# Four float32 column-tile products in place of three fp32r products in the attention's projections

## The chip, the cores and the metric

The kernel runs on one core of a Trainium2 chip, as one program of five engines: TensorE (PE, matrix products), VectorE (DVE), ScalarE (ACT), GpSimd (POOL) and SyncE (SP, which here issues every DMA). The engines run side by side and meet by semaphores. The metric is the device time of one execution in microseconds (us), lower is better.

## What is computed

The reference, cut to what matters. The input `x` is (2, 2048, 512) in float32.

```python
def _mhsa(X, ln_g, ln_b, Wq, bq, Wk, bk, Wv, bv, Wo, bo):       # 16 heads of 32
    Xn = (X - mu) * rsqrt(var + EPS) * ln_g + ln_b
    Q, K, V = (split_heads(Xn @ W + b) for W, b in ((Wq, bq), (Wk, bk), (Wv, bv)))
    scores = einsum('bhqd,bhkd->bhqk', Q, K) / sqrt(32)          # causal mask
    AV = einsum('bhqk,bhkd->bhqd', softmax(scores), V)
    return AV.swapaxes(-2, -3).reshape(...) @ Wo + bo

def _ffn(x, ...):                                                # fp4 weights, 512 -> 2 x 1408 -> 512
    gate, up = split(x @ w_gu.T)
    y = (silu(gate) * up) @ w_down.T
    return y / sqrt(mean(y * y) + 1e-6)

x = x + 0.5 * _ffn(_layernorm(x))
x = x + _mhsa(_layernorm(x))
x = x + 0.5 * _ffn(_layernorm(x))
```

## The kernel before

The program has eight stages in a row on every engine (`tensor_program` and its like): the first FFN over 8 token tiles of 512 (`Ffn` with phase 0, which also decodes the weights and keeps them in DRAM as `dg` and `dd`), then for each of two batches the projections Q, K, V (`Qkv`), the attention (`Att`) and the output projection (`Out`), and last the second FFN. Each stage has an order written out once (`order`), which every engine walks through and of which it takes its own steps; waits are explicit (`wait_ge` on a named signal at a key). A step of one engine queues behind all its earlier steps.

**Projections.** A projection is a product of 512 by 512. The PE multiplies fp32r operands, and to keep precision each operand is split into a high part (the value rounded to fp32r) and a low part (the rest), and a product is the sum of three matmuls, high x high, high x low and low x high, accumulated in one PSUM bank. This goes for Xn (`xh`, `xl`), Wq, Wk, Wv (`wh`, `wl`), the attention's result (`Out.ah`, `al`) and Wo (`Out.wh`, `wl`). The contraction of 512 is four chunks of 128 rows, `c` from 0 to 3, so one output tile of 128x512 is twelve matmuls (`qkv_project`, `out_pe`).

For each token tile `tt` of 512 (four per batch), `Qkv.order` gives: eight feature tiles (K and Q in turn, 128 features by 512 tokens) and between them the 48 VectorE steps of the next token tile's two norms; then four value tiles (128 tokens by 512 features), each followed by one `turn` of the next token tile. A `turn` is one chunk of Xn: PE transposes four 128x128 blocks into bank 0 or 1, ScalarE applies gain and bias and writes `xnt`, VectorE copies it to `xh` and subtracts for `xl`. Before token tile 0 the four turns stand alone with three `split` steps, in which ScalarE rounds a weight of 128x2048 to `wh` and VectorE subtracts for `wl`. A finished feature tile is copied by ScalarE to `q32` (with bias), cast to fp16 by VectorE and its rest made by GpSimd. The value tiles of token tile 3 are not done there but in the attention's order, in 16 parts of one chunk each (`value_part`), each followed by one `max` unit.

**Attention.** For each group of four heads and each query tile, PE makes scores twice: once for the row maxima (`max`, VectorE reduces them), once transposed for the exponential (`score`, ScalarE). It needs copies of Q and K stacked by DMA (`stack_sp`). `weigh` multiplies the exponentials by V and `total` sums them, both in float32 with 32 stationary columns per head, the four heads to the four quarters of 32 partitions of one bank:

```python
for j in range(4):
    h = 4 * hg + j
    e.wait_ge(*t.exp_done.at((b, n, j)))
    k = e.matmul(AV[32 * j:32 * j + 32, off:512], p.v[:, kt, 32 * h:32 * h + 32],
                 t.E[n % NE][:, j, off:512], start=kt == 0, stop=kt == 4 * qt + 3)
```

The order mixes `max` units and small steps (`parts`: `invert`, VectorE's reciprocals, and the splits `wo_split` and `av_split`) into the scores by a count of work, in `advance`. `wo_split` splits Wo after step (2, 3, 0), `av_split` the first 512 tokens of the result after step (3, 2, 2).

**Output.** `out_pe` makes 16 tiles of 128 tokens by 512. The splits of the tokens 512 to 2047 stand in `out_act` and `out_dve`. VectorE adds residual and bias (`y_made`) and does the next stage's norm beside it; SP stores the tile. In batch 1, SP also loads the second FFN's weights: for each of 11 column blocks one piece of gate and up (`dg`) and one of down (`dd`), 512 KB each, where their memory is free. Blocks 4 to 7 of `dg` wait for the end, since `Out.wh` and `Out.wl` lie there, and blocks 5 to 8 of `dd` for tile 11, since `ah[0]` and `al[0]` lie there.

## Time and profile before

| | us |
|---|---|
| median of three runs | 2980.32 |
| lowest and highest | 2968.59, 2982.92 |
| the profiled execution | 2964.9 |
| its span | 2963.1 |

| busy in the span | us | share |
|---|---|---|
| PE matmul | 2716.4 | 92% |
| PE weight load (beside matmuls) | 1623.7 | 55% |
| VectorE | 2157.6 | 73% |
| ScalarE | 1381.1 | 47% |
| GpSimd | 1494.4 | 50% |

Rows of the timeline give the start in us from the span's start, the busy time of the merged instructions, the engine, the line of the helper that issued them, the operation with its operands and shape, and in brackets how long the engine was idle before and for whom it waited. `pp` and `ps` are PSUM banks, `sb` is SBUF. "128*32 128x512 f32" is a matmul with 128 rows and 32 stationary columns, and 512 columns that stream through. fp32r operands are shown as f32 too; the three products of the projections are the "128*128 128x512 f32". Busy time holds the modelled end of the last matmul, so the distance between two starts tells more than it does. PEld is the load of stationary operands.

### The profile page before, as it was taken

To read this page: it belongs to the slowest core of one execution; us is meant where nothing else is said; L and a number is where in the kernel's file an instruction comes from. 1 tells how busy PE (TensorE), PEld (TensorE's weight loads), DVE (VectorE), ACT (ScalarE), POOL (GpSimd) and SP (SyncE) were. 2 spreads that over 40 slices of the span, in tenths; PEclk is the share of its full clock that TensorE was granted. 3 is DMA by queue.
4 is the path that set the end of the run, shared out by engine and by line. 5 is a ranking of instruction groups with operands and counts; after the bars stand their busy time and mean duration, and the time that the engine had idled before them with its cause. 6 is when DMAs were issued, how large, how long until landed. Compare 5 with 4: busy or idle time off the path is not lost.

```text
span 2963.1 us, 39754 instructions
## 1 busy us (share of the span) xinstructions
PE 2716.4 (92%) x14559; PEld 1623.7 (55%) x14559; DVE 2157.6 (73%) x3834; ACT 1381.1 (47%) x2667; POOL 1494.4 (50%) x1015
## 2 busy tenths in 40 slices
PE   6799999997998999988899899999988999999998
PEld 4677777775773333322277523332324777777776
DVE  8877777777758777777287587777763777777765
ACT  4444554544213555555522245555554354544554
POOL 5555555553222665555732145555557355555554
PEclk8999999998999999999999999999999999999999
DMA  2022201121022010200140300211003401111101
GB/s 58 15 88 75 113 33 35 43 81 62 29 50 54 5 45 5 59 5 2 37 150 29 89 16 5 45 30 35 4 3 141 172 15 43 43 43 43 43 29 43
DMA packets 75713, 142.12 MB, mean 48 GB/s; under 512 B 18783, under 2 KB 22394, under 8 KB 75390
## 3 DMA queue, kind: packets, MB, share of 16 engines
q1 hardware_dynamic: 75518, 139.58, 15.0%
q8 instruction: 115, 1.88, 0.3%
q14 instruction: 80, 0.66, 0.1%
HBM read 74.00 MB, written 37.22 MB: 38 GB/s over the span
## 4 chain that ended last, share of the span: by engine, by line
PE 55%; DVE 22%; ACT 9%; issue 6%; POOL 2%; SPq 1%; DMA 1%; POOLq 0%; ACTq 0%; DVEq 0%
PE pp L94 42%; PE ps L94 13%; DVE sb L109 9%; ACT sb L100 8%; DVE sb L115 3%; DVE sb L106 3%; DVE sb L103 2%; DVE sb L121 2%; POOL sb L103 2%; SPq L133 1%; DVE sb L118 1%; DVE sb L112 1%; DMA sb<-xa 1%; PE ps L97 0%; DVE sb L124 0%
## 5 line engine op out<-in xcount | busy, mean ns | idle before, releaser
L94 PE MATMUL pp<-sb,sb 128*128 128x512 f32 (+8 forms) x11154 | 2221.4, 435 | 130.3 <-ACT sb L100 33.9
L103 POOL TENSOR_TENSOR sb<-sb,sb 128x512 f32<-128x512 f32 (+6 forms) x998 | 1486.9, 1507 | 1453.4 <-ACT sb L100 594.1
L94 PEld LDWEIGHTS pp<-sb,sb 128*128 128x128 f32 (+3 forms) x11154 | 1196.3, 143 | 855.8 <-ACT sb L100 196.7
L100 ACT ACTIVATE sb<-pp 128x512 f32<-128x512 f32 (+4 forms) x1434 | 674.2, 548 | 546.7 <-PE pp L94 528.7
L94 PE MATMUL ps<-sb,sb 128*128 128x512 f32 (+5 forms) x2862 | 765.9, 362 | 72.3 <-DVE sb L109 25.1
L100 ACT ACTIVATE sb<-sb 128x512 f32<-128x512 f32 (+3 forms) x468 | 300.9, 649 | 680.2 <-DVE sb L109 559.5
L94 PEld LDWEIGHTS ps<-sb,sb 128*128 128x128 f32 (+3 forms) x2862 | 382.0, 148 | 413.7 <-DVE sb L115 197.8
L115 DVE TENSOR_REDUCE sb<-ps 128x1 f32<-128x512 f32 (+3 forms) x754 | 488.4, 670 | 156.4 <-PE ps L94 154.7
L109 DVE SCALAR_TENSOR_TENSOR sb<-ps,sb,sb 128x512 f32<-128x512 f32 x437 | 321.5, 745 | 139.1 <-PE ps L94 121.3
L109 DVE SCALAR_TENSOR_TENSOR sb<-pp,sb,sb 128x512 f32<-128x512 f32 x443 | 324.4, 743 | 119.6 <-PE pp L94 106.2
L115 DVE TENSOR_REDUCE sb<-pp 128x1 f32<-128x512 f32 (+2 forms) x366 | 243.0, 664 | 80.2 <-PE pp L94 79.5
L100 ACT ACTIVATE sb<-pp,sb 128x512 f32<-128x512 f32 x325 | 218.7, 678 | 135.7 <-PE pp L94 114.7
L100 ACT ACTIVATE sb<-ps,sb 128x512 f32<-128x512 f32 x299 | 198.1, 686 | 94.6 <-PE ps L97 90.2
L118 DVE RECIPROCAL sb<-pp 128x64 f32<-128x64 f32 x256 | 114.5, 508 | 99.0 <-PE pp L94 99.0
L103 DVE TENSOR_TENSOR sb<-sb,sb 128x512 fp32r<-128x512 f32 (+4 forms) x165 | 131.6, 822 | 8.8 <-ACT sb L100 6.5
L109 DVE SCALAR_TENSOR_TENSOR sb<-sb 128x4 f32<-128x4 f32 x288 | 106.2, 369 | 6.1
L106 DVE TENSOR_SCALAR sb<-sb 128x4 int32<-128x4 int32 (+2 forms) x233 | 91.7, 410 | 24.4 <-ACT sb L100 20.4
L103 DVE TENSOR_TENSOR sb<-pp,sb 128x512 f32<-128x512 f32 (+1 forms) x95 | 65.0, 688 | 52.4 <-PE pp L94 30.1
L112 DVE CAST sb<-sb 128x512 f16<-128x512 f32 (+2 forms) x128 | 58.6, 458 | 57.6 <-ACT sb L100 56.3
L100 ACT ACTIVATE sb<-ps 128x512 fp32r<-128x512 f32 (+1 forms) x73 | 43.0, 591 | 113.3 <-PE ps L94 73.5
L121 DVE BATCH_NORM_STATS2 sb<-sb 128x6 f32<-128x512 f32 x128 | 86.6, 677 | 11.6 <-DMA sb<-L_attn_X 6.5
L109 DVE SCALAR_TENSOR_TENSOR sb<-sb,sb,sb 128x512 f32<-128x512 f32 x64 | 79.5, 1282 | 0.5
(19 smaller groups left out, 360.9 us busy)
## 6 DMA issues: line engine op xcount, KB each, us to landing
sb<-sb SPq DMA_DIRECT2D x192, 128.0 KB, 2.4
sb<-L_attn_X SPq DMA_DIRECT2D x64, 256.0 KB, 4.0
sb<-xa SPq DMA_DIRECT2D x64, 256.0 KB, 5.3
sb<-xc SPq DMA_DIRECT2D x64, 256.0 KB, 4.3
xa<-sb SPq DMA_DIRECT2D x32, 256.0 KB, 2.0
xc<-sb SPq DMA_DIRECT2D x32, 256.0 KB, 3.7
out<-sb SPq DMA_DIRECT2D x32, 256.0 KB, 2.0
dg<-sb SPq DMA_DIRECT2D x11, 512.0 KB, 8.7
```

What stands on the lines that cost most here:

```text
L94: return self.e.matmul(*a, **k) if self.e else self
L100: return self.e.activation(*a, **k) if self.e else self
L103: return self.e.tensor_tensor(*a, **k) if self.e else self
L106: return self.e.tensor_scalar(*a, **k) if self.e else self
L109: return self.e.scalar_tensor_tensor(*a, **k) if self.e else self
L112: return self.e.tensor_copy(*a, **k) if self.e else self
L115: return self.e.reduce_max(*a, **k) if self.e else self
L118: return self.e.reciprocal(*a, **k) if self.e else self
L121: return self.e.bn_stats(*a, **k) if self.e else self
L133: return self.e.dma_start(*a, **k) if self.e else self
```

## The change

All splits of the four projections are gone, with their buffers and signals. A chunk of a product is now `product`: four float32 matmuls, each with 32 of the 128 stationary columns, written to the quarter of 32 partitions that belongs to these columns. ScalarE writes Xn straight to `xnt`, now a whole token tile and double, and takes over the waits for its memory. The weights are multiplied as they are loaded. SP loads Wq, Wk and Wv for batch 0 together, once the first FFN's token tile 6 has left their memory. The attention's order loses `wo_split` and `av_split`, eight subtractions and eight copies per batch, and `Out` loses twelve of each. As less memory is taken in the output, SP loads 20 pieces of the second FFN's weights with the first ten stores of batch 1, and two, `dg` of blocks 2 and 3, after the last store.

```diff
--- before.py
+++ after.py
@@ -815,35 +815,31 @@
             q = p.qkv
             e.wait_ge(*f.turned.at((NT - 1, KC - 1)))
             q.load_sp(e, 0, 0)
-            e.wait_ge(*f.gu_done.at((0, IC - 1, KC - 1, 1)))
-            for n in (1, 0):
+            e.wait_ge(*f.gu_done.at((NT - 2, IC - 1, KC - 1, 0)))
+            for n in (1, 0, 2):
                 q.weight_sp(e, 0, n)
-    if f.ph == 0:
-        e.wait_ge(*f.stored.at(NT - 1))
-        p.qkv.weight_sp(e, 0, 2)
-    else:
-        e.wait_ge(*f.stored.at(NT - 1))
+    e.wait_ge(*f.stored.at(NT - 1))
+
+
+def product(e, out, left, right, start, stop):
+
+    for j in range(0, 128, 32):
+        k = e.matmul(out[j:j + 32, :], left[:, j:j + 32], right, start=start, stop=stop)
+    return k
 
...
 class Qkv:
     def __init__(self, p):
         self.p = p
-        self.raw = [[p.at([128, KC, D], F32, o) for o in raw]
-                    for raw in ((A0 + 24576, A0 + 32768, XR0), (C0 + 8192, C0, XR0))]
         o = QS0 + 32768
-        self.wh = [p.at([128, KC, D], F32R, o + 16384 * i) for i in range(3)]
-        self.wl = [p.at([128, KC, D], F32R, o + 16384 * i + 8192) for i in range(3)]
-        self.xnt = [p.at([128, 512], F32, KP0 + 16384 + 2048 * i) for i in range(2)]
+        self.w = [p.at([128, KC, D], F32, o + 8192 * i) for i in (1, 0, 2)]
         self.q32 = [p.at([128, 512], F32, KP0 + 20480 + 2048 * i) for i in range(2)]
-        xo = [KP0, o + 49152]
-        self.xh = [p.at([128, KC, 512], F32R, xo[i]) for i in range(2)]
-        self.xl = [p.at([128, KC, 512], F32R, xo[i] + 8192) for i in range(2)]
+        self.xnt = [p.at([128, KC, 512], F32, x) for x in (KP0, o + 49152)]
         self.x_in = p.sign("q_x_in", 16)
         self.w_in = [p.sign(f"q_w_in{n}", 16) for n in range(3)]
-        names = ("normed", "turned", "xnt_made", "xh_made", "xl_made", "wh_made", "wl_made", "proj_done", "q_wide",
-                 "q_hi", "q_lo", "v_made")
-        (self.normed, self.turned, self.xnt_made, self.xh_made, self.xl_made, self.wh_made, self.wl_made,
-         self.proj_done, self.q_wide, self.q_hi, self.q_lo, self.v_made) = (p.sign("q_" + x) for x in names)
+        names = ("normed", "turned", "xnt_made", "proj_done", "q_wide", "q_hi", "q_lo", "v_made")
+        (self.normed, self.turned, self.xnt_made, self.proj_done, self.q_wide, self.q_hi, self.q_lo, self.v_made) = (
+            p.sign("q_" + x) for x in names)
         self.src = p.xa.rearrange("(b n t p) d -> b n t p d", b=B, t=4, p=128)
...
-        e.dma_start(self.raw[b][n][:, :, :], w).then_inc(*self.w_in[n].up(b))
+        e.dma_start(self.w[n][:, :, :], w).then_inc(*self.w_in[n].up(b))
...
     def order(self, b):
-        yield "turn", 0, 0
-        yield "turn", 0, 1
-        yield "split", 1
-        yield "turn", 0, 2
-        yield "turn", 0, 3
-        yield "split", 0
-        yield "split", 2
+        for c in range(KC):
+            yield "turn", 0, c
         yield "load", 1
...
     for c in range(KC):
-        e.wait_ge(*q.xl_made.at((b, tt, c)))
-        e.matmul(bank, lh(c), rh(c), start=c == 0, stop=False)
-        e.matmul(bank, lh(c), rl(c), start=False, stop=False)
-        k = e.matmul(bank, ll(c), rh(c), start=False, stop=c == KC - 1)
+        e.wait_ge(*q.xnt_made.at((b, tt, c)))
+        k = product(e, bank, left(c), right(c), c == 0, c == KC - 1)
         if c < KC - 1:
             yield
     k.then_inc(*q.proj_done.up((b, *key)))
...
-    e.wait_ge(*q.wl_made.at((b, 2)))
-    yield from qkv_project(e, p, b, tt, ("values", tt, tb), lambda c: q.xh[i][:, c, c0], lambda c: q.xl[i][:, c, c0],
-                           lambda c: q.wh[2][:, c, :], lambda c: q.wl[2][:, c, :])
+    e.wait_ge(*q.w_in[2].at(b))
+    yield from qkv_project(e, p, b, tt, ("values", tt, tb), lambda c: q.xnt[i][:, c, c0], lambda c: q.w[2][:, c, :])
...
         if what == "turn":
             tt, c = at
             e.wait_ge(*q.turned.at((b, tt, c)))
-            if tt or c >= 2:
-                last = (b, tt, c - 2) if c >= 2 else (b, tt - 1, c + 2)
-                e.wait_ge(*q.xl_made.at(last))
+            if tt >= 2:
+                e.wait_ge(*q.proj_done.at((b, "values", tt - 2, 3)))
+            elif tt == 1 and b:
+                for s in p.out.stored:
+                    e.wait_ge(*s.at((0, 3)))
             elif b == 0:
                 e.wait_ge(*p.f[0].w_out.at("all"))
-            e.activation(q.xnt[c % 2][:, :], p.b[c % 2], ACT.Identity, scale=p.bias[:, 0, c:c + 1],
+            e.activation(q.xnt[tt % 2][:, c, :], p.b[c % 2], ACT.Identity, scale=p.bias[:, 0, c:c + 1],
                          bias=p.bias[:, 1, c:c + 1]).then_inc(*q.xnt_made.up((b, tt, c)))
-        elif what == "split":
-            n = at[0]
-            e.wait_ge(*q.w_in[n].at(b))
-            if n == 2 and b:
-                for s in p.out.stored[0:2]:
-                    e.wait_ge(*s.at((0, 3)))
-            if n == 0:
-                e.wait_ge(*q.wl_made.at((b, 1)))
-            e.activation(q.wh[n][:, :, :], q.raw[b][n][:, :, :], ACT.Copy).then_inc(*q.wh_made.up((b, n)))
...
     q = p.qkv
     gens = {}
     for what, *at in q.order(b):
-        if what == "turn":
-            tt, c = at
-            i = tt % 2
-            e.wait_ge(*q.xnt_made.at((b, tt, c)))
-            if c == 0 and tt >= 2:
-                e.wait_ge(*q.proj_done.at((b, "values", tt - 2, 3)))
-            elif c == 0 and tt == 1 and b:
-                for s in p.out.stored:
-                    e.wait_ge(*s.at((0, 3)))
-            elif c == 0 and tt == 0 and b == 0:
-                e.wait_ge(*p.f[0].w_out.at("all"))
-            e.tensor_copy(q.xh[i][:, c, :], q.xnt[c % 2][:, :]).then_inc(*q.xh_made.up((b, tt, c)))
-            e.wait_ge(*q.xh_made.now())
-            e.tensor_tensor(q.xl[i][:, c, :], q.xnt[c % 2][:, :], q.xh[i][:, c, :], ALU.subtract).then_inc(
-                *q.xl_made.up((b, tt, c)))
-        elif what == "split":
-            n = at[0]
-            e.wait_ge(*q.wh_made.at((b, n)))
-            e.tensor_tensor(q.wl[n][:, :, :], q.raw[b][n][:, :, :], q.wh[n][:, :, :], ALU.subtract).then_inc(
-                *q.wl_made.up((b, n)))
...
             if n < N:
                 if steps[n] == (2, 1, 0):
                     out.append(("wo",))
-                if steps[n] == (2, 3, 0):
-                    parts += [("wo_split", c) for c in range(KC)]
-                if steps[n] == (3, 2, 2):
-                    parts += [("av_split", 0, c) for c in range(KC)]
...
-        self.wraw = p.at([128, KC, D], F32, C0 + 8192)
-        self.wh, self.wl = (p.at([128, KC, D], F32R, C0 + 16384 + 8192 * i) for i in range(2))
-        self.ah = [p.at([128, KC, 512], F32R, x) for x in (KP0, o)]
-        self.al = [p.at([128, KC, 512], F32R, x + 8192) for x in (KP0, o)]
+        self.w = p.at([128, KC, D], F32, C0 + 8192)
         self.xr = [[p.at([128, 512], F32, (o + 32768 if i < 12 or b == 0 else XR0 - 24576) + 2048 * i)
                     for i in range(16)] for b in range(B)]
         self.w_in = p.sign("o_w_in", 16)
         self.x_in = [p.sign(f"o_x_in{n}", 16) for n in range(16)]
         self.stored = [p.sign(f"o_stored{q}", 16) for q in range(4)]
-        (self.wh_made, self.wl_made, self.ah_made, self.al_made, self.biased, self.done, self.y_made) = (
-            p.sign("o_" + x) for x in ("wh_made", "wl_made", "ah_made", "al_made", "biased", "done", "y_made"))
...
-def out_wo_act(e, p, b, c):
-    o = p.out
-    e.wait_ge(*o.w_in.at(b))
-    e.activation(o.wh[:, c, :], o.wraw[:, c, :], ACT.Copy).then_inc(*o.wh_made.up((b, c)))
...
-def out_wo_dve(e, p, b, c):
-    o = p.out
-    e.wait_ge(*o.wh_made.at((b, c)))
-    e.tensor_tensor(o.wl[:, c, :], o.wraw[:, c, :], o.wh[:, c, :], ALU.subtract).then_inc(*o.wl_made.up((b, c)))
...
-def out_split_act(e, p, b, q, c):
-    o = p.out
-    e.wait_ge(*p.att.normed.at((b, c, q)))
-    if q >= 2:
-        e.wait_ge(*o.done.at((b, 4 * (q - 2) + 3)))
-    elif q == 1:
-        e.wait_ge(*p.att.exp_done.at((b, 159, 3)))
-    else:
-        e.wait_ge(*p.att.exp_done.at((b, p.att.last_step(2), 3)))
-    e.activation(o.ah[q % 2][:, c, :], p.avn[:, c, 512 * q:512 * q + 512], ACT.Copy).then_inc(*o.ah_made.up((b, q, c)))
-
-
-def out_split_dve(e, p, b, q, c):
-    o = p.out
-    e.wait_ge(*o.ah_made.at((b, q, c)))
-    e.tensor_tensor(o.al[q % 2][:, c, :], p.avn[:, c, 512 * q:512 * q + 512], o.ah[q % 2][:, c, :],
-                    ALU.subtract).then_inc(*o.al_made.up((b, q, c)))
...
+        e.wait_ge(*o.w_in.at(b))
         for c in range(KC):
-            e.wait_ge(*o.al_made.at((b, q, c)))
-            e.wait_ge(*o.wl_made.at((b, c)))
-            e.matmul(p.b[n % 8], o.ah[i][:, c, c0], o.wh[:, c, :], start=c == 0, stop=False)
-            e.matmul(p.b[n % 8], o.ah[i][:, c, c0], o.wl[:, c, :], start=False, stop=False)
-            k = e.matmul(p.b[n % 8], o.al[i][:, c, c0], o.wh[:, c, :], start=False, stop=c == KC - 1)
+            e.wait_ge(*t.normed.at((b, c, q)))
+            k = product(e, p.b[n % 8], p.avn[:, c, 128 * n:128 * n + 128], o.w[:, c, :], c == 0, c == KC - 1)
...
         q, tb = divmod(n, 4)
-        if tb == 0 and q < 3:
-            for c in range(KC):
-                out_split_dve(e, p, b, q + 1, c)
...
     for n in range(16):
         e.wait_ge(*p.f[0].stored.at(4 * b + n // 4))
         e.dma_start(o.xr[b][n][:, :], o.src[b, n // 4, n % 4]).then_inc(*o.x_in[n].up(b))
-    e.wait_ge(*o.wl_made.at((b, 3)))
     if b == 0:
         for n in (1, 0, 2):
             p.qkv.weight_sp(e, 1, n)
     else:
         e.wait_ge(*p.f[0].w_out.at("all"))
-    first = [x for i in (0, 1, 2, 3, 4, 8, 9, 10) for x in ((i, 0), (i, 1)) if x not in ((4, 0), (8, 1))]
+    first = [x for i in range(IC) for x in ((i, 0), (i, 1)) if x not in ((2, 0), (3, 0))]
     for n in range(16):
         if b == 1:
             for i, u in first[2 * n:2 * n + 2]:
                 load_piece_sp(e, p, f, i, u)
-            if n == 12:
-                e.wait_ge(*o.done.at((1, 11)))
-                for i in range(5, 9):
-                    load_piece_sp(e, p, f, i, 1)
         e.wait_ge(*o.y_made.at((b, n)))
         e.dma_start(o.dst[b, n // 4, n % 4], o.xr[b][n][:, :]).then_inc(*o.stored[n // 4].up((b, 3)))
     if b == 1:
-        for i in range(4, 8):
+        for i in range(2, 4):
             load_piece_sp(e, p, f, i, 0)
```

On PE at the start of the projections of batch 0, the order before (`sb_141` and `sb_143` are the high and low part of Wk, `sb_132` and `sb_135` those of Xn):

```order
L97 MATMUL ps<-sb_49,sb_102 128x128
L97 MATMUL ps<-sb_49,sb_103 128x128
L94 MATMUL pp<-sb_141,sb_132 128x512
L94 MATMUL pp<-sb_143,sb_132 128x512
L94 MATMUL pp<-sb_141,sb_135 128x512
```

And now, with `sb_126` Wk, `sb_125` Wq, `sb_127` Wv and `sb_130` Xn:

```order
L97 MATMUL ps<-sb_49,sb_102 128x128
L97 MATMUL ps<-sb_49,sb_103 128x128
L94 MATMUL pp<-sb_130,sb_126 32x512 x16
L94 MATMUL pp<-sb_130,sb_125 32x512 x16
L94 MATMUL pp<-sb_130,sb_126 32x512 x16
```

Twelve matmuls per tile have become sixteen of 32 rows of output.

On VectorE late in the attention of batch 0 (`sb_161` is the low part of the attention's result, the other rows are maxima and reciprocals), before:

```order
L118 RECIPROCAL sb_149<-pp 128x64
L115 TENSOR_REDUCE sb_151<-ps 128x1
L118 RECIPROCAL sb_149<-pp 128x64 x7
L103 TENSOR_TENSOR sb_161<-sb_118,sb_159 128x512 x4
L115 TENSOR_REDUCE sb_151<-pp 128x1
L115 TENSOR_REDUCE sb_151<-ps 128x1 x2
```

And now:

```order
L118 RECIPROCAL sb_136<-pp 128x64
L115 TENSOR_REDUCE sb_138<-ps 128x1
L118 RECIPROCAL sb_136<-pp 128x64 x7
L115 TENSOR_REDUCE sb_138<-pp 128x1
L115 TENSOR_REDUCE sb_138<-ps 128x1 x2
```

The four subtractions between the reciprocals and the next maxima are gone; the rest stands as it stood.

## Rows read from the trace of the kernel before

**Rows 1.** The page: its span, and the chain that ended last by engine.
```profile
span 2963.1 us, 39754 instructions
...
PE 55%; DVE 22%; ACT 9%; issue 6%; POOL 2%; SPq 1%; DMA 1%; POOLq 0%; ACTq 0%; DVEq 0%
```

**Rows 2.** Busy times in the attention of batch 0; columns stand in the first line.
```profile
core 0: us, PE busy (x) PEld busy (x) DVE busy (x) ACT busy (x) POOL busy (x), PEclk, DMA share, GB/s
...
894.00:1472.00 578.00, 535.64 (x3723) 173.33 (x3727) 415.65 (x716) 313.47 (x680) 324.43 (x175) 0.98 0.10 23
```

**Rows 3.** Timeline of PE: fp32r products in the output of batch 0.
```profile
1484.22 16.48 PE L94 MATMUL pp<-sb,sb 128*128 128x512 f32 x72
1500.54 5.60 PE L94 MATMUL ps<-sb,sb 128*128 128x512 f32 x24
```

**Rows 4.** Timeline of PE and PEld: float32 matmuls with 32 columns in the attention.
```profile
1195.38 1.07 PE L94 MATMUL pp<-sb,sb 128*32 128x512 f32 x8
1196.38 0.39 PE L94 MATMUL ps<-sb,sb 96*128 96x512 f16 x1
...
1465.02 0.16 PEld L94 LDWEIGHTS pp<-sb,sb 128*32 128x32 f32 x8 [0.21 <-issue]
1465.48 0.13 PEld L94 LDWEIGHTS pp<-sb,sb 128*32 128x32 f32 x4 [0.30 <-POOL sb L103]
1465.91 0.13 PEld L94 LDWEIGHTS pp<-sb,sb 128*32 128x32 f32 x4 [0.30 <-issue]
...
1465.91 1.04 PE L94 MATMUL pp<-sb,sb 128*32 128x512 f32 x8
```

**Rows 5.** Timeline of PE: start of Q, K, V in batch 0.
```profile
723.14 1.78 PE L97 MATMUL ps<-sb,sb 128*128 128x128 f32 x8 [3.53 <-ACT sb L100]
732.01 27.15 PE L94 MATMUL pp<-sb,sb 128*128 128x512 f32 x108 [7.08 <-DVE sb L103]
760.52 1.60 PE L97 MATMUL ps<-sb,sb 128*128 128x128 f32 x4 [1.36 <-DVE sb L106]
...
764.74 0.60 PE L97 MATMUL ps<-sb,sb 128*128 128x128 f32 x4
765.09 3.00 PE L94 MATMUL pp<-sb,sb 128*128 128x512 f32 x12
```

**Rows 6.** Timeline of PE: ends of Q, K, V in both batches, and batch 1's start.
```profile
870.31 0.52 PE L94 MATMUL ps<-sb,sb 96*128 96x128 f16 x6
872.98 0.29 PE L94 MATMUL ps<-sb,sb 96*128 96x128 f16 x2 [2.15 <-DMA sb<-sb]
...
1523.44 1.09 PE L97 MATMUL ps<-sb,sb 128*128 128x128 f32 x8 [0.97 <-DVE sb L103]
...
1664.27 0.52 PE L94 MATMUL ps<-sb,sb 96*128 96x128 f16 x6
1668.03 0.29 PE L94 MATMUL ps<-sb,sb 96*128 96x128 f16 x2 [3.24 <-DMA sb<-sb]
```

**Rows 7.** Timeline of PE: one part of V and the unit behind it.
```profile
882.93 0.95 PE L94 MATMUL pp<-sb,sb 128*128 128x512 f32 x3
883.72 0.45 PE L94 MATMUL ps<-sb,sb 96*128 96x512 f16 x2
```

**Rows 8.** Timeline of PE and DVE: two waits in the attention of batch 0.
```profile
1297.71 2.48 PE L94 MATMUL pp<-sb,sb 128*32 128x512 f32 x9 [2.73 <-DVE sb L118]
...
1393.83 7.29 DVE L103 TENSOR_TENSOR sb<-sb,sb 128x512 fp32r<-128x512 f32 x4 [0.75 <-ACT sb L100]
...
1401.78 0.61 PE L94 MATMUL pp<-sb,sb 96*128 96x512 f16 x1 [4.01 <-DVE sb L115]
```

**Rows 9.** Timeline of PE: starts of both outputs and the end of the second.
```profile
1476.34 8.05 PE L94 MATMUL ps<-sb,sb 128*128 128x512 f32 x24 [3.87 <-DVE sb L118]
...
2271.64 8.03 PE L94 MATMUL ps<-sb,sb 128*128 128x512 f32 x24 [3.87 <-DVE sb L118]
...
2317.89 1.03 PE L97 MATMUL ps<-sb,sb 128*128 128x128 f32 x8
```

**Rows 10.** DMA issues: count, KB each, median us from issue to landing.
```profile
sb<-dg SPq DMA_DIRECT2D x11, 512.0 KB, 7.5
```

More of the change, by code:

```diff
@@ L1348, in att_act @@
                     *t.av_kept.up((b, hg, qt)))
-        elif what == "wo_split":
-            out_wo_act(e, p, b, at[0])
-        elif what == "av_split":
-            out_split_act(e, p, b, *at)
 def att_dve(e, p, b):
@@ L1389, in att_dve @@
             e.reciprocal(t.rec[:, x], p.b[7][:, x]).then_inc(*t.inverted.up((b, hg, qt, c)))
-        elif what == "wo_split":
-            out_wo_dve(e, p, b, at[0])
-        elif what == "av_split":
-            out_split_dve(e, p, b, *at)
     t.max_red.mark((b, "end"))
@@ L1436, in att_sp @@
                 e.wait_ge(*t.stacked[1][j].at((b, 3)))
-            e.dma_start(p.out.wraw[:, :, :], p.a["L0_attn_Wo"].rearrange("(c p) n -> p c n", p=128)).then_inc(
+            e.dma_start(p.out.w[:, :, :], p.a["L0_attn_Wo"].rearrange("(c p) n -> p c n", p=128)).then_inc(
                 *p.out.w_in.up(b))
@@ L1453, in __init__ @@
         self.stored = [p.sign(f"o_stored{q}", 16) for q in range(4)]
[L1454 to L1455 removed]
+        self.biased, self.done, self.y_made = (p.sign("o_" + x) for x in ("biased", "done", "y_made"))
         self.src = p.xa.rearrange("(b n t p) d -> b n t p d", b=B, t=4, p=128)
@@ L1527, in out_dve @@
         q, tb = divmod(n, 4)
-        if tb == 0 and q < 3:
-            for c in range(KC):
-                out_split_dve(e, p, b, q + 1, c)
         x = o.xr[b][n][:, :]
```

17 lines of the change are left out of this document (5 added, 12 removed).

## The prediction, made before the changed kernel ran

> **What bounds the kernel now.** I read the page's chain of work first: TensorE (PE) holds 55% of it, more than the other engines together [rows 1]. Then the busy times by stage: even in the attention of one batch, the stage with the most exchange between engines, PE is busy 535.64 of 578 us [rows 2]. In the projections it is nearly unbroken. So in the stages that the change touches the end is set by how long PE needs for a product, plus the few places where PE stands idle for work that the change removes. The order of this part is: the price of one product, the projections Q, K, V, the attention, the output, the edges.
>
> **One product.** A projection tile is 128x512 over four chunks of 128. Before, a chunk is three fp32r matmuls of 128 columns. 72 of them in a row start at 1484.22 and the next group starts at 1500.54 [rows 3]: 16.32/72 = 0.227 us each, 0.68 per chunk, 2.72 per tile. After, a chunk is four fp32 matmuls with 32 stationary columns each. The trace of before has this very form: the attention's `weigh` and `total` steps are four fp32 matmuls of 128x32 against 512 columns, written to the four partition quarters of one bank. The trace records each as two matmuls, so a group of four is eight records, in two batches of four. Where `weigh` and `total` stand back to back, the loads of the batches start at 1465.02 (two batches' at once), 1465.48 and 1465.91 and matmuls with them [rows 4]: 0.43 us a batch, **0.86 us a chunk**, 3.44 per tile. A single group between other matmuls takes 1195.38 to 1196.38, 1.00 us [rows 4]; the 0.14 more is paid only where PE changes between this form and another. So a tile costs 0.72 us more than before, a chunk 0.18. There are 48 tiles per batch in Q, K, V and 16 in the output, 128 in all, 512 chunks: +92 us if nothing else moved.
>
> The four weight loads for the last batch run from 1465.91, together with matmuls at 1465.91, and are over in 0.13 us [rows 4]; no time is lost for them. The Trainium skill (page "TensorE: Matmul & The Clock Gate", Part 3, on what overlaps) says that a weight load overlaps running matmuls only where its row group differs, and column tiles share all rows. By that rule each batch would pay its load, and the sum would be 1024 x 0.13 = 133 us higher. The rows contradict it for this form.
>
> **Q, K, V of batch 0.** Before: from the transposes of chunks 2 and 3 at 723.14 to the last tile's end, where attention's first units start at 870.31 [rows 5, 6], 147.2 us. In it, PE waits 7.08 us for the hi/lo splits of activations and weights on ScalarE and VectorE before the first product at 732.01, and the first 108 matmuls last until 760.52, 28.5 us instead of 24.5, of which some 1.7 are the wait for the next norm (the row's 1.36 and its edge) and 2.3 a TensorE clock that is still low. After: no split stands between. The products wait for the scaled transposes alone (`xnt_made`), which ScalarE makes with one operation each, and for the weights, loaded during the last token tile of the FFN. So: transposes 1.8 (723.14 [rows 5]), low clock 2.3 as before, three token tiles of 8 x 3.44 for Q and K and 4 x (3.44 + 0.35 for the transposes [rows 5] + 0.14 for the change of form) = 43.2, that is 129.7, the last eight tiles 27.5, a first part of V 1.0: 162.3, **+15.1**. The waits for norms (1.36 in [rows 5], two more like it) vanish, since VectorE has the same norms in 27.5 instead of 21.8 us and no splits; at that rate its norm would have to take 6 us longer to be late again.
>
> **Batch 1.** Before: 1523.44 to 1664.27 [rows 6], 140.8. After: 2.6 until the last transpose (batch 0's 1.8, and 0.8 since here the first pair is not turned yet), low clock between 0 and 2.3, I take 0.5 because PE came busy from the output, then 129.7 + 27.5 + 1.0: 161.3, **+20.5**. At token tile 1 the scaled transpose on ScalarE now waits for the sixteen stores of batch 0, and its copies of Q and K queue behind it; but the last store is let go by the same sum as the transposes at 1523.44, some 30 us before, so it costs nothing.
>
> **The copies for attention.** After the last Q/K tile PE waits for the stacked head copies, 2.15 and 3.24 us [rows 6]. They are issued once the second Q/K tile of token tile 3 is stored, and PE now has six tiles of 3.44 before it needs them, 4.3 us more. Both waits go: **-5.4**.
>
> **V of token tile 3** runs in 16 chunk parts per batch, each between fp16 units. A part costs 0.79 before (882.93 to 883.72 [rows 7]), of which 0.11 is already an exposed change of weights; after it costs the 1.00 of a single group: +0.21 x 15 x 2 = 6.3. The low clock behind the two waits just removed cost about 1.0 each: **+4.3**.
>
> **Attention.** VectorE's splits of Wo and of the first 512 columns of the attention result fall into it, on engines that other work queues behind. Four subtractions at 1393.83 take 7.29 us, since GpSimd uses the same memory at that time, and PE waits 4.01 us until 1401.78 for a maximum that stands behind them [rows 8]. Four others push the reciprocals back, and PE waits 2.73 for them at 1297.71 [rows 8], where other such places cost about 1. Four ScalarE copies between exponentials cost another 1.0. I take back 4.1 + 1.8 + 1.0 = 6.9 per batch, **-13.8**. It reaches the end because PE is 93% busy there [rows 2]. Ends: nothing (another maximum is late in their place) and -20.
>
> **Output.** Before: 1476.34 to 1523.44 and 2271.64 to 2317.89 [rows 6, 9], 47.1 and 46.3. PE starts when the last reciprocals are in; this stays. After: 16 x 3.44 = 55.0, low clock 2.4 as now (24 matmuls from 1476.34 to 1484.22, 7.9 instead of 5.4 [rows 3, 9]), 1.1 for the last addition in batch 0: 58.5 and 57.6, **+22.7**. The splits of each quarter leave VectorE and ScalarE, but no wait of PE's stood on them here beyond 1 us.
>
> **Edges at nothing.** Wv is loaded earlier. In the output of batch 1 the queue loads 20 of the 22 weight pieces of the second FFN beside the stores, and the last two, gate/up of column blocks 2 and 3, after the last store; before, these were blocks 4 to 7. They land 7.5 us after issue [rows 10], and PE needs block 2 only after two blocks of work, over 12 us. If the fuller queue delayed the stores, which the second FFN waits for, it would cost 0 to 3 us.
>
> **Sum.** 15.1 + 20.5 - 5.4 + 4.3 - 13.8 + 22.7 = **+43.4 us**. The profiled execution took 2964.9 with a span of 2963.1, 15 below the median 2980.32 of three runs (2968.59 to 2982.92). 3008.3/2964.9 = 1.0146, on the median 3024.
>
> **Rivals.**
> (a) The batch is slower in long streams. The first two batches of each group in the trace stand 0.46 apart (1465.02 to 1465.48 [rows 4]). If one of the two batches of every chunk costs that, +0.03 x 512 = +15; if both do, +31, and 3055. For it: PE now takes 8 loads and 8 matmuls per 0.86 us for 27 us on end, which no stretch of before shows. Against: the third and fourth batch keep 0.43. 15%.
> (b) The groups don't join: each chunk costs the 1.00 of a single one, because each starts on another weight chunk. +0.14 x 512 = 72, 3096. Against: `total` follows `weigh` with other weights, another operand and another bank, and joins. 7%. With the rule on weight loads, 3157: 2%.
> (c) The other side, faster than before: in `weigh` the four tiles read four different moving operands, in a projection one and the same. If reading set the 0.43, a batch could take less. At 0.39 a batch (0.775 a chunk, 43.4/512 less) the kernel is level; at 0.34, the price of the three fp32r matmuls, it gains 92 against the sum and ends at 2932. Against: 0.43 is just under two times the 0.227 of one fp32r matmul of the same 512 columns [rows 3], so it looks like two passes of the columns through the array, not like reading. 3%.
> (d) No change: the chip gives back 28 us more than I found, in attention (maxima and exponentials closer together) and in the clock, 2965 to 2995. For it: PE is idle 42 of the attention's 578 us [rows 2], and I take back 6.9. Against: the 28 us would have to come from waits that the change does not touch. 5%.
>
> **Numbers.** My forecast holds 68%, with 3005 to 3045. (a) adds the stretch to 3055. Range 3000 to 3060: it leaves out (b), (c), (d), 17%, and a few per cent at the edges of the others. About 0.5% (15 us) is what a measurement of this kernel can tell from no change: slower 0.91, same 0.06 ((d) and the low edge of the first case), faster 0.03.
>
> **What would show it.** In the profile after: eight-record groups starting every 0.86 us in Q, K, V; evacuations of Q and K by ScalarE 3.44 us apart where they were 2.72; the first product some 2 us after the transposes instead of 6 to 9; no DMA wait before attention; no fp32r subtraction and no 4 us wait in attention; output about 57.5 us. It is wrong if that distance isn't 3.44, or if the attentions don't shorten.

## The result, and the profile after

The changed kernel takes 3016.68 us (median of 4 runs, 3009.46 to 3023.44), the kernel before 2974.45 (4 runs, 2967.64 to 2982.92): a ratio of 1.014, interval 1.0095 to 1.0185. Forecast were 1.0146 and 3024 us. The profiled execution took 3011.0 us with a span of 3009.2, against 2964.9 and 2963.1.

The page of the kernel after, its chain by engine (of before: [rows 1]):

```profile
span 3009.2 us, 44657 instructions
...
PE 65%; DVE 15%; ACT 8%; issue 5%; POOL 2%; DMA 0%; SPq 0%; POOLq 0%; ACTq 0%; DVEq 0%
```

TensorE holds ten points more of the chain, and VectorE seven less, whose subtractions are gone. The stages, by the starts of PE's instructions at their borders (the last column is the prediction's sum, its -5.4 and +4.3 set to the stage they belong to):

| stage | before, us | after, us | difference | forecast |
|---|---|---|---|---|
| first FFN | 723.1 | 725.6 | +2.4 | 0 |
| Q, K, V, batch 0 | 147.2 | 163.5 | +16.3 | +15.1 |
| units and parts of V ahead of the attention | 20.8 | 21.8 | +1.0 | 0.0 |
| attention, batch 0 | 585.2 | 576.2 | -9.0 | -6.9 |
| output, batch 0 | 47.1 | 57.6 | +10.5 | +11.4 |
| Q, K, V, batch 1 | 140.8 | 163.5 | +22.7 | +20.5 |
| units and parts of V | 21.9 | 21.8 | -0.1 | -1.1 |
| attention, batch 1 | 585.4 | 574.5 | -11.0 | -6.9 |
| output, batch 1 | 46.3 | 57.7 | +11.4 | +11.3 |
| second FFN | 645.2 | 647.1 | +1.9 | 0 |
| sum | 2963.1 | 3009.2 | +46.1 | +43.4 |

**The price of a product.** Timeline of PE after, the output of batch 0 (against [rows 3, 9]):

```profile
1487.01 8.77 PE L94 MATMUL ps<-sb,sb 128*32 128x512 f32 x64 [3.96 <-DVE sb L118]
1495.57 20.81 PE L94 MATMUL pp<-sb,sb 128*32 128x512 f32 x192
1516.17 7.08 PE L94 MATMUL ps<-sb,sb 128*32 128x512 f32 x64
```

The middle group starts at 1495.57 and the next at 1516.17: 20.60 us for 192 records, 24 chunks of eight, **0.858 us a chunk** where 0.86 was forecast. The first 64 records, eight chunks, take 8.56 instead of 6.87: the low clock behind the wait of 3.96.

**Start of Q, K, V.** Timeline of PE after, batch 0 and then batch 1 (against [rows 5, 6]):

```profile
725.56 1.79 PE L97 MATMUL ps<-sb,sb 128*128 128x128 f32 x8 [3.53 <-ACT sb L100]
727.28 32.12 PE L94 MATMUL pp<-sb,sb 128*32 128x512 f32 x288
759.32 0.66 PE L97 MATMUL ps<-sb,sb 128*128 128x128 f32 x4
759.91 3.64 PE L94 MATMUL pp<-sb,sb 128*32 128x512 f32 x32
763.48 0.66 PE L97 MATMUL ps<-sb,sb 128*128 128x128 f32 x4
764.07 3.64 PE L94 MATMUL pp<-sb,sb 128*32 128x512 f32 x32
...
1544.65 1.09 PE L97 MATMUL ps<-sb,sb 128*128 128x128 f32 x8 [0.81 <-DVE sb L103]
...
1547.43 2.78 PE L94 MATMUL pp<-sb,sb 128*32 128x512 f32 x24
```

The first product stands 1.7 us behind the transposes, where it was 8.9, and the waits for a norm ahead of the transposes (759.32) are gone. What the forecast missed is in the next rows: four transposes between column-tile products take 0.59 us (763.48 to 764.07) instead of 0.35 [rows 5], and the value tile behind them 3.57.

**Into the attention.** Timeline of PE after (against [rows 6, 7]):

```profile
889.04 0.64 PE L94 MATMUL ps<-sb,sb 96*128 96x128 f16 x8
889.61 1.06 PE L94 MATMUL pp<-sb,sb 128*32 128x512 f32 x8
890.61 0.51 PE L94 MATMUL ps<-sb,sb 96*128 96x256 f16 x4
```

All eight scores run together: no DMA wait after the sixth. A part of V takes 1.00 (889.61 to 890.61), as forecast.

**The attention.** Busy time of PE in both attentions, of the kernel before and then of the one after (columns: window, its length, busy time, granted clock, DMA share, GB/s):

```profile
891.14:1476.34 585.20, 536.51 (x3728) 0.98 0.10 24
1686.19:2271.64 585.45, 536.49 (x3728) 0.98 0.10 24
```

```profile
910.82:1487.01 576.19, 533.23 (x3729) 0.99 0.10 24
1729.96:2304.41 574.45, 531.76 (x3728) 0.99 0.10 24
```

Idle time went down by 5.7 and 6.3 us, and busy time by 3.3 and 4.7, with the same instructions. The waits of PE in the attention of batch 0 that changed, before and then after (us in total, times, longest):

```profile
PE pp L94 <- DVE sb L115: 6.4, 10, 4.0
PE pp L94 <- DVE sb L118: 4.5, 4, 2.7
```

```profile
PE pp L94 <- DVE sb L115: 2.6, 10, 0.6
PE pp L94 <- DVE sb L118: 2.2, 3, 1.2
```

These are the two waits of [rows 8]; nothing of their size took their place.

### The profile page after: what moved, and what is told of

Read it like the earlier page. It is cut to its first block, busy times and chain, and to the rows that moved or that the text cites. A ratio compares the mean times of both kernels' runs of the same rounds, so it can differ in the third digit from the quotient of the medians.

```text
span 3009.2 us, 44657 instructions
## 1 busy us (share of the span) xinstructions
PE 2796.5 (93%) x17119; PEld 1462.8 (49%) x17119; DVE 2060.9 (68%) x3724; ACT 1349.3 (45%) x2621; POOL 1489.0 (49%) x1015
## 3 DMA queue, kind: packets, MB, share of 16 engines
q1 hardware_dynamic: 75518, 139.58, 14.7%
## 4 chain that ended last, share of the span: by engine, by line
PE 65%; DVE 15%; ACT 8%; issue 5%; POOL 2%; DMA 0%; SPq 0%; POOLq 0%; ACTq 0%; DVEq 0%
PE pp L94 51%; PE ps L94 13%; ACT sb L100 8%; DVE sb L109 8%; DVE sb L115 3%; POOL sb L103 2%; DVE sb L106 1%; DVE sb L118 1%; DVE sb L103 1%; PE ps L97 1%; DVE sb L121 1%; DVE sb L112 1%; DMA sb<-sb 0%; SPq L133 0%; DVE sb L124 0%
## 5 line engine op out<-in xcount | busy, mean ns | idle before, releaser
L94 PE MATMUL pp<-sb,sb 128*32 128x512 f32 (+9 forms) x13554 | 2286.1, 483 | 105.6 <-ACT sb L100 31.2
L94 PEld LDWEIGHTS pp<-sb,sb 128*32 128x32 f32 (+4 forms) x13554 | 1045.5, 128 | 1024.2 <-issue 422.3
L94 PE MATMUL ps<-sb,sb 128*128 128x512 f32 (+7 forms) x3022 | 768.7, 384 | 70.3 <-DVE sb L109 26.6
L94 PEld LDWEIGHTS ps<-sb,sb 128*128 128x128 f32 (+4 forms) x3022 | 370.9, 144 | 446.0 <-DVE sb L115 218.0
L100 ACT ACTIVATE sb<-sb 128x512 fp32r<-128x512 f32 (+4 forms) x422 | 266.4, 632 | 629.4 <-DVE sb L109 562.4
L106 DVE TENSOR_SCALAR sb<-sb 128x4 int32<-128x4 int32 (+2 forms) x233 | 96.9, 432 | 24.4 <-ACT sb L100 20.5
L112 DVE CAST sb<-sb 128x512 f16<-128x512 f32 (+1 forms) x96 | 47.2, 491 | 83.5 <-ACT sb L100 82.3
L106 DVE TENSOR_SCALAR sb<-sb,sb,sb 128x512 f32<-128x512 f32 x128 | 79.5, 652 | 0.5
```

What stands on the lines that cost most here:

```text
L94: return self.e.matmul(*a, **k) if self.e else self
L100: return self.e.activation(*a, **k) if self.e else self
L106: return self.e.tensor_scalar(*a, **k) if self.e else self
L112: return self.e.tensor_copy(*a, **k) if self.e else self
```

## The experiments

All ratios are to the kernel before, run on the same chip beside them. A single profiled execution can be some 13 us longer through its first FFN alone (last section), so traces are compared by stage.

**Is 0.858 a price of the column tiles?** `e1_full` multiplies all 128 columns at once, `e2_wide64` takes two tiles of 64.

```diff
-    for j in range(0, 128, 32):
-        k = e.matmul(out[j:j + 32, :], left[:, j:j + 32], right, start=start, stop=stop)
-    return k
+    return e.matmul(out, left, right, start=start, stop=stop)
```

> The changed kernel with each float32 chunk as one matmul of all 128 stationary columns instead of four of 32. The changed kernel's profiled run took 3011.0 us, a chunk 0.858. Theory of passes: float32 needs four passes of the 512 columns whatever the number of stationary columns, 0.853 us; the four tiles run beside each other, so they gain nothing in the array, and what differs is the load of the stationary operand. If the load of 128 float32 columns hides behind the matmuls, the time is the same within 10 us; if it stands between them (a load took 0.15 to 0.19 us in the kernel before, one per two passes), a chunk costs up to 1.2 us and the kernel 3011 + 0.3 x 512 = 3165. Rival: a 128-column float32 matmul is not four passes but the tiles serve something else, a chunk under 0.8 and the kernel under 2985. I expect 3011 to 3060, and that the forms of 32 columns buy only the hidden loads.

> The changed kernel with two float32 matmuls of 64 stationary columns per chunk instead of four of 32. Passes: a chunk stays at 0.86 and the kernel at 3011 within 10 us, with half the instructions. If the number of instructions in flight sets the 0.43 us of a batch, it falls below 0.40 here and the kernel gains 30 us or more. If 64-column tiles don't run side by side, a chunk costs 1.7 us and the kernel 3450.

Measured: `e1_full` 2997.04 us (2995.41 to 3007.57), ratio 1.0082, interval 1.005 to 1.0114; `e2_wide64` 3017.99 us (3011.59 to 3024.39), ratio 1.0145 from two runs. The middle group of the output of batch 0, of `e1_full` and of `e2_wide64`:

```profile
1498.75 20.76 PE L94 MATMUL pp<-sb,sb 128*128 128x512 f32 x48
1519.35 1.02 PE L94 MATMUL ps<-sb,sb 128*128 128x512 f32 x2
```

```profile
1495.73 20.79 PE L94 MATMUL pp<-sb,sb 128*64 128x512 f32 x96
1516.33 1.04 PE L94 MATMUL ps<-sb,sb 128*64 128x512 f32 x4
```

All three forms take 20.60 us for 24 chunks. So the price belongs to float32: a chunk is 3.8 times one fp32r matmul of the same 512 columns [rows 3], and four narrow matmuls side by side cost what one wide one does. Four times as many weight loads change nothing in the stream. What the tiles do cost is at their edges. `e1_full` in Q, K, V of batch 0:

```profile
774.08 0.60 PE L97 MATMUL ps<-sb,sb 128*128 128x128 f32 x4
774.52 3.60 PE L94 MATMUL pp<-sb,sb 128*128 128x512 f32 x8
777.95 0.60 PE L97 MATMUL ps<-sb,sb 128*128 128x128 f32 x4
```

Transposes and a value tile take 3.87 us there (774.08 to 777.95), in the changed kernel 4.16 (759.32 to 763.48). Q, K, V are 159.0 and 159.9 us long instead of 163.5 twice, and the parts of V ahead of the attention 19.1 instead of 21.8 and 21.8. That is some 13.5 us in all, and the attention and the output are as long in both within 2 us. The two ratios' intervals just overlap, but the stages decide: the wide form is the better one by these 13 us, which I had not expected, though it is slower than the kernel before.

**Does the shared moving operand matter?** `e3_rotate` lets the four tiles of a bank read four different chunks at a time, in Q, K, V and in the output; the edit for Q, K, V:

```diff
-    for c in range(KC):
-        e.wait_ge(*q.xnt_made.at((b, tt, c)))
-        k = product(e, bank, left(c), right(c), c == 0, c == KC - 1)
+    e.wait_ge(*q.xnt_made.at((b, tt, KC - 1)))
+    for s in range(KC):
+        for j in range(4):
+            c, x = (s + j) % KC, slice(32 * j, 32 * j + 32)
+            k = e.matmul(bank[x, :], left(c)[:, x], right(c), start=s == 0, stop=s == KC - 1)
...
```

> The changed kernel with the chunks rotated over the four column tiles: in one group tile j multiplies chunk (s + j) mod 4, so that the four tiles read four different moving operands, as in the attention, and not the same one. The sum is the same. Rival (c) of the prediction, that shared reading matters, in either direction: a chunk then changes from 0.858. Passes: 0.858 stays, the kernel stays within 5 us of 3011, and only the first product of a token tile starts up to 1 us later, since it waits for all four chunks.

Measured: 3024.47 us (3018.59 to 3030.35), ratio 1.0166 from two runs, some 8 us above the changed kernel. Not by the products, as a value tile and the next ones show:

```profile
763.31 3.64 PE L94 MATMUL pp<-sb,sb 128*32 128x512 f32 x32
766.88 0.66 PE L97 MATMUL ps<-sb,sb 128*128 128x128 f32 x4
...
772.65 5.79 PE L94 MATMUL pp<-sb,sb 128*32 128x512 f32 x52 [0.96 <-ACT sb L100]
```

The tile takes the same 3.57 us. But each token tile's first product now needs the last scaled transpose, and PE waits 0.96 us for ScalarE behind the transposes, four times per batch, 3.8 us in all: Q, K, V are 168.7 and 167.7 us long. So reading has no part in the price, and the edit brought a wait of its own that I had not counted.

**The two halves of the change.** `e7_out_only` has the output in column tiles and no splits for it, with the old Q, K, V; `e8_qkv_only` the opposite, with the old attention and output.

`e7_out_only` against before:

```diff
-                if steps[n] == (2, 3, 0):
-                    parts += [("wo_split", c) for c in range(KC)]
-                if steps[n] == (3, 2, 2):
-                    parts += [("av_split", 0, c) for c in range(KC)]
...
+            k = product(e, p.b[n % 8], p.avn[:, c, 128 * n:128 * n + 128], o.w[:, c, :], c == 0, c == KC - 1)
...
```

`e8_qkv_only` against before (the parts of the attention's result, `ah` and `al`, also lie elsewhere, where their memory is free):

```diff
...
-        e.matmul(bank, lh(c), rh(c), start=c == 0, stop=False)
-        e.matmul(bank, lh(c), rl(c), start=False, stop=False)
-        k = e.matmul(bank, ll(c), rh(c), start=False, stop=c == KC - 1)
+        e.wait_ge(*q.xnt_made.at((b, tt, c)))
+        k = product(e, bank, left(c), right(c), c == 0, c == KC - 1)
...
```

> One part alone: the output projection in float32 column tiles, with no splits in attention and output, while Q, K, V keep three fp32r products and splits. Theory: the two outputs cost +10.5 and +11.4, the attentions give back 9 and 11: 2964.9 + 2 = 2967, no difference from the kernel before that can be measured. Rival: the attention's gain is tied to the projections' change (another phase of the clock or of GpSimd); then +20.

> The other part alone: Q, K, V in float32 column tiles, attention and output with their splits as before. Theory: the whole loss of the change is here: +16.3 and +22.7 in the projections, about +1 around the first units of attention, 2964.9 + 40 = 3005. Rival: the parts don't add up, this one costs under 30 or over 50.

Measured: `e7_out_only` 2978.26 us (2967.68 to 2983.74, 12 runs), ratio 0.9994, interval 0.9976 to 1.0012; `e8_qkv_only` 3020.99 us (3009.29 to 3021.89), ratio 1.0141, interval 1.0119 to 1.0163. In the first the attentions are 10.2 and 10.6 us shorter and the outputs 11.7 and 11.4 longer. In the second Q, K, V are 163.5 us long in both batches, as in the changed kernel, and the attentions with their first units 606.8 and 608.8, where the kernel before has 606.0 and 607.4. The loss of the whole change lies in Q, K, V; in the output the products cost what the attention gives back.

**What the splits cost the attention.** `e6_splits_back` adds the eight splits per batch to the changed kernel again, with nobody using their results. `e4_spread` is the kernel before with them one at a time, at four steps of the order instead of four in a row.

`e6_splits_back` against after:

```diff
+                if steps[n] == (2, 3, 0):
+                    parts += [("wo_split", c) for c in range(KC)]
+                if steps[n] == (3, 2, 2):
+                    parts += [("av_split", 0, c) for c in range(KC)]
...
```

`e4_spread` against before:

```diff
-                if steps[n] == (2, 3, 0):
-                    parts += [("wo_split", c) for c in range(KC)]
-                if steps[n] == (3, 2, 2):
-                    parts += [("av_split", 0, c) for c in range(KC)]
+                if steps[n][0:2] == (2, 3) and kt in (4, 7, 10, 13):
+                    parts += [("wo_split", (kt - 4) // 3)]
+                if steps[n][0:2] == (3, 3) and kt in (4, 7, 10, 13):
+                    parts += [("av_split", 0, (kt - 4) // 3)]
```

> The changed kernel with the eight copies and eight subtractions of Wo and of the attention's result back in each attention, at their old places; their results are not used. Theory: the attentions get 9 and 11 us longer again, the kernel 3011 + 20 = 3031. Rival: the gain came from elsewhere (the output's start, the clock): under 5 us in both together.

> The kernel before with its three fp32r products and all its splits, but the eight splits in each batch's attention spread out: one of Wo each after key tiles 4, 7, 10, 13 of step (2, 3), one of the result each after the same of step (3, 3), instead of four in a row. Theory: the attention of the changed kernel got 9 and 11 us shorter because a row of four subtractions beside GpSimd (7.3 us) kept maxima and reciprocals waiting; single ones of 0.7 to 2 us fit beside PE's work. Then this kernel gains 5 to 9 us per batch on the one before, 2950 instead of 2964.9. Rival: what counts is VectorE's whole work, or the shared memory access; then it gains under 3 us.

Measured: `e6_splits_back` 3044.34 us (3029.69 to 3045.22), ratio 1.0218, interval 1.0194 to 1.0242; `e4_spread` 2965.91 us (2954.45 to 2969.95, 12 runs), ratio 0.9965, interval 0.9946 to 0.9985. Busy time of PE in the attentions of `e6_splits_back`, where the waits of the kernel before are back, and two of its waits in batch 0:

```profile
911.81:1497.38 585.57, 536.21 (x3728) 0.98 0.10 24
1740.88:2326.59 585.71, 536.08 (x3728) 0.98 0.10 24
```

```profile
PE pp L94 <- DVE sb L115: 6.3, 10, 4.0
PE pp L94 <- DVE sb L118: 4.3, 3, 2.7
```

Against the changed kernel the attentions are 9.4 and 11.3 us longer: 6.4 and 6.9 idle, 3.0 and 4.3 busy. So the splits alone account for what the attention gave, though not which of them, ScalarE's copies or VectorE's subtractions. The span is 21.7 us longer than the changed kernel's, where 20 was expected. The busy part is the clock. Windows behind the two waits of [rows 8] in the kernel before:

```profile
1297.00:1301.00 4.00, 3.29 (x13) 0.50 0.00 0
1401.00:1406.00 5.00, 4.22 (x13) 0.50 0.00 0
```

The granted clock is 0.50, the lower of the two levels, 1.2 GHz: after waits of 2.7 and 4.0 us the matmuls that follow run at that level. In the kernel after the clock stays at 1.00 from 1300 to 1480:

```profile
1300.00:1480.00 180.00, 167.30 (x1180) 1.00 0.01 3
```

Spreading the splits gives 4.9 and 4.6 us per batch back (units included), about half of what leaving them out does. One wait of PE for VectorE grew instead, from 0.7 us to 3.35; it is for a subtraction of 128x16 between the last row maxima of a group and the next scores:

```profile
1422.08 0.58 PE L94 MATMUL ps<-sb,sb 128*32 128x128 f16 x4 [3.35 <-DVE sb L103]
```

**Would Q, K, V gain from missing splits at the old price?** `e5_three` makes three fp32r products of the high parts alone and no low parts in Q, K, V, while ScalarE still rounds the weights. Without the low parts its output is not the reference's.

```diff
-        e.wait_ge(*q.xl_made.at((b, tt, c)))
-        e.matmul(bank, lh(c), rh(c), start=c == 0, stop=False)
-        e.matmul(bank, lh(c), rl(c), start=False, stop=False)
-        k = e.matmul(bank, ll(c), rh(c), start=False, stop=c == KC - 1)
+        e.wait_ge(*q.xnt_made.at((b, tt, c)))
+        for r in range(3):
+            k = e.matmul(bank, lh(c), rh(c), start=c == 0 and r == 0, stop=c == KC - 1 and r == 2)
...
```

> The kernel before without the low parts in Q, K, V: twelve fp32r matmuls per tile stay, but all three of a chunk multiply high part by high part, so VectorE makes no low parts of activations or weights there (ScalarE still rounds the weights); its output is not the reference's. Attention and output are as before. It has the changed kernel's freedom from splits with the old product, and so takes the projections' change apart. Theory: per batch the projections stage is 192 chunks (179 until the attention's first units) x 0.178 = 32 us shorter than in the changed kernel (163.5), near 132, against 147.2 and 140.8 before; so the waits for splits were worth some 15 and 9 us of the kernel before, and the product costs 32 more. Kernel 2964.9 - 24 - 2 = about 2939. Rival: the stage is set by something else, evacuation or norms on VectorE; then it stays above 138 in both batches.

Measured: 2971.48 us (2958.82 to 2979.89, 10 runs), ratio 0.9973, interval 0.9956 to 0.999. That is a clear miss: Q, K, V are 146.4 and 137.9 us long, where 132 was expected, against 147.2 and 140.8 before. The wait for the splits does go: the first product of batch 0 starts at 740.39, 2.6 us behind the transposes at 737.84. ScalarE in batch 0, and then PE:

```profile
750.05 1.92 ACT L100 ACTIVATE sb<-sb 128x2048 fp32r<-128x2048 f32 x1 [6.66 <-DMA sb<-L_attn_Wv]
751.87 1.24 ACT L100 ACTIVATE sb<-pp,sb 128x512 f32<-128x512 f32 x2
...
773.16 1.84 PE L97 MATMUL ps<-sb,sb 128*128 128x128 f32 x4 [5.70 <-DVE sb L106]
```

ScalarE still rounds Wv there, and waits 6.66 us for its load, which SP issues late. The first copies of K and Q queue behind that, VectorE's casts behind the copies, its next norm behind the casts, and PE waits 5.70 us for the norm. The kernel before has the same load, hidden by splits that take as long:

```profile
735.65 1.91 ACT L100 ACTIVATE sb<-sb 128x2048 fp32r<-128x2048 f32 x1 [1.75 <-DMA sb<-L_attn_Wv]
```

In batch 1 of `e5_three` ScalarE does not wait for Wv, but PE still waits three times for a norm (us in total, times, longest):

```profile
PE ps L97 <- DVE sb L106: 3.4, 3, 1.3
```

The changed kernel has no such wait in either batch. So what hides the norms there is the longer product: at the old length the missing splits leave these waits in place, and are worth 2.9 us in batch 1. The earlier load of Wv is not what the change lives on. Nothing rounds Wv in it, and its first value tile starts 34.4 us behind the transposes (725.56 to 759.91), while the late load was there after 12.5 (723.14 to 735.65). How long Q, K, V of batch 0 would be at the old price without the rounding too was not tried.

**A version that beats both.** `e9_mixed` is the kernel before, but the first four output tiles of a batch are plain float32 products from `avn` and the unsplit Wo, and meanwhile ScalarE and VectorE split Wo and the next 512 tokens. The loads that reuse Wo's memory move behind tile 3.

```diff
-                if steps[n] == (2, 3, 0):
-                    parts += [("wo_split", c) for c in range(KC)]
-                if steps[n] == (3, 2, 2):
-                    parts += [("av_split", 0, c) for c in range(KC)]
...
+        for c in range(KC if n < 4 else 0):
+            e.wait_ge(*t.normed.at((b, c, 0)))
+            k = e.matmul(p.b[n], p.avn[:, c, c0], o.wraw[:, c, :], start=c == 0, stop=c == KC - 1)
```

> The kernel before, with the eight splits per batch taken out of the attention: the first four output tiles of a batch are float32 products of 128 columns from the unsplit operands, and meanwhile ScalarE and VectorE split Wo and the tokens 512 to 1023; the other twelve tiles stay fp32r. Theory (the splits cost the attention about 10 us per batch by the waits they cause, wherever their engines serve PE): the attention with its first units takes 596 us per batch instead of 606 and 607, the output 47.1 + 4 x 0.72 = 50 and 49.2, together -21 + 6 = -15 us, a ratio of 0.995. Rival (the work only moves): VectorE needs eight subtractions during the 13.8 us of the four tiles; at the 1.8 us each that four of them took in the attention of the kernel before, 14.6 us, PE waits some 3 us before tile 4 or more, and the ratio is 0.997 to 0.998, like that of the spread-out splits. Slower than before would mean that a weight piece or a load that had to move is late.

Measured: 2963.65 us (2948.67 to 2968.45, 12 runs) against 2976.3 (17 runs), ratio 0.9961, interval 0.9941 to 0.9981. PE in its output of batch 0, and VectorE beside it:

```profile
1464.77 8.72 PE L94 MATMUL ps<-sb,sb 128*128 128x512 f32 x16 [3.87 <-DVE sb L118]
1473.33 17.92 PE L94 MATMUL pp<-sb,sb 128*128 128x512 f32 x64
1491.09 5.60 PE L94 MATMUL ps<-sb,sb 128*128 128x512 f32 x24
...
1464.32 10.19 DVE L103 TENSOR_TENSOR sb<-sb,sb 128x512 fp32r<-128x512 f32 x8
```

The eight subtractions take 10.19 us, less than the four tiles, and PE does not wait for them. The attentions are 9.5 and 9.1 us shorter (from the first units on), the outputs 1.9 and 1.9 longer. Its span of 2946.9 stands against 2963.1, with first FFNs of the same length (719.2 and 718.6 to the transposes). Of these 16.2 us, 14.7 lie in attention and output; Q, K, V of batch 0, whose code is the same, are 2.7 shorter. Like `e4_spread` it is faster than both kernels beyond its interval; which of these two is the better, 0.9961 or 0.9965, the ratios do not decide. The stages speak for `e9_mixed`: its 14.7 us in attention and output stand against 9.6 in `e4_spread`.

## Why the prediction was right

**One product: right.** 0.858 against 0.86, 0.68 before, so the 512 chunks cost (0.858 - 0.681) x 512 = 91 us; the forecast had 92. Rivals (a) and (b) fall with this number. So does the rule on weight loads of the Trainium skill (page "TensorE: Matmul & The Clock Gate", Part 3): by it a chunk would have cost 0.26 more (two batches, 0.13 each), 1.12 us. The fp32r products of the kernel before contradict it as well: they start 0.227 us apart, and each has a weight load that takes 0.188 beside it (72 products of the output of batch 0; busy us, mean ns of one, idle before):

```profile
L94 PEld LDWEIGHTS pp<-sb,sb 128*128 128x128 f32 x71 | 13.3, 188 | 2.8
```

Rival (c) falls with `e3_rotate` and `e1_full`: neither another moving operand nor a single wide matmul changes the price.

**Q, K, V: right in kind, 1.2 and 2.2 us short.** The step that failed is "4 x (3.44 + 0.35 for the transposes + 0.14 for the change of form)". The change of form is paid twice, once on the way into the transposes and once out: 4.16 instead of 3.93, 0.23 x 12 = 2.8 us per batch. In batch 0 the low clock at the start gave 1.1 of it back (32.04 us for the first 36 chunks, less 36 x 0.858, is 1.2, where 2.3 was taken). Norm waits, the split waits and the stack waits went as said; by `e5_three` the norm waits went for the first of the two reasons given, the longer product, and not for the missing splits. That batch 0 came so near is in part luck of the profile compared with: the same code takes 144.6, 144.7 and 144.5 us in `e4_spread`, `e7_out_only` and `e9_mixed`, and against these the loss is 18.7 to 19.0 us and not 16.3.

**V and the copies: near, by two misses.** A part costs the 1.00 of the forecast. But the two small scores ahead of it, whose second waits for the change of form, take 0.38 instead of 0.26 (a part with its unit is 1.38 us apart from the next, before 1.05), so the step "+0.21 x 15 x 2" should have been +0.33, 3.6 us more. The clock behind the removed DMA waits gave back more than the 1.0 each that I took: the first three parts of V behind the wait of batch 0 take 4.78 us in the kernel before (873.08 to 877.86), at a granted clock of 0.72, and 3.20 in `e5_three` (887.00 to 890.20), at 1.00, so 1.6. Over both batches the units and parts changed by +0.8 us, where -5.4 + 4.3 = -1.1 was forecast.

**Attention: the right waits, a size off.** Forecast -13.8, measured -20.0. Idle time gave 12.0, near the 4.1 + 1.8 + 1.0 per batch that I took back. The other 8.0 are the matmuls behind those waits, which ran at the 0.50 clock. I had counted that term for the output and the start of Q, K, V, and not here. It could have been read in advance: a window behind the wait at 1401.78 [rows 8] shows it.

**Output: right.** +10.5 and +11.4 against +11.4 and +11.3. In batch 0 the low clock took 1.7 us (8.56 less 6.87) and not 2.4. The 57.6 of batch 1 was added up wrongly: its terms, 55.0 and 2.4, make 57.4.

**Edges: right, with one reservation.** The second FFN waits for the same things as long in both (VectorE 13.8 us in 6 waits, 8.4 in 20), so the moved weight pieces cause no wait. Yet the stage is tied to the change: it takes 646.4 to 647.1 us in all six kernels with a float32 output (the changed one, `e1_full`, `e2_wide64`, `e3_rotate`, `e6_splits_back`, `e7_out_only`) and 645.2 to 645.8 in the five whose output ends in fp32r products, `e9_mixed` among them. The clock does not account for it: it is 0.97 instead of 1.00 in the first 60 us of the changed kernel's second FFN, but 1.00 in `e6_splits_back`, which takes 646.9. The cause of this 1 us or so stays open. The early load of Wv did cost nothing. Rival (d), no change, had asked for 28 us more from attention and clock; 6.2 came.

The misses, +3.4 in Q, K, V, +1.9 in V and units, -6.2 in the attention, -0.8 in the output, +4.3 in the two FFNs, of which the first's 2.4 have nothing to do with the change (`e3_rotate` has the same first FFN and takes 722.7), leave 2.7 us. That the sum came out so near is in part luck: the terms were right within 1 to 3 us each, apart from the attention.

## What to carry to other kernels

Take the price of a new form of matmul from wherever the kernel already runs it back to back, and add the change of form at each border where two forms meet, in both directions. When a wait of PE is removed, count the slow matmuls behind it with the wait: here they were worth two thirds as much again, 8.0 us on 12.0. And before replacing splits by a dearer product everywhere, look where the splits stand: the cheap places are where their engines are idle, and a few dear products can be the cover for them, as in `e9_mixed`.

## What the runs showed of the hardware

- Float32 costs 0.858 us per 128 rows, 128 stationary and 512 moving columns, in one, two or four column tiles. Three fp32r products cost 0.68. So dropping the splits can pay only where the waits that go with them come to more than 0.18 us per chunk.
- Column tiles cost at their borders: four transposes between them 0.59 us, between wide float32 products 0.44, between fp32r products 0.35; a single chunk between fp16 matmuls 1.00, the wide one 0.91.
- The first FFN is the same in all kernels, yet Q, K, V's first transposes start at 718.1 to 721.8 us in seven profiled executions and at 732.7 to 733.3 in four. The difference is PE's clock early on: from 60 to 80 us it is 1.00 in the seven, and 0.84, 0.72, 0.74 and 0.85 in the four (`e1_full`, `e4_spread`, `e5_three`, `e7_out_only`). Why it differs from one execution to the next is not known. The same window in `e7_out_only` and in the kernel before:

```profile
60.00:80.00 20.00, 13.24 (x51) 0.85 0.00 0
```

```profile
60.00:80.00 20.00, 15.44 (x77) 1.00 0.00 1
```

Two groups show in the unprofiled runs as well: of the 17 times of the kernel before beside `e9_mixed`, eight are 2965 to 2971 us and nine 2976 to 2984. The "15 below the median" of the prediction is most likely this, since its profile was of the shorter kind; the other runs left no trace. A difference of under 15 us between two spans says nothing here; the stages do.
